# A fused four-layer kernel: the order of the first loads, and of the third pair's products

## What is computed

```
x = x + x @ W0[id0[b]] + b0[id0[b]]                      # one of 16 experts
x = x + x @ W1.T + s[a] * (x @ A[a].T) @ Bm[a].T          # W1, and one of 8 adapters, a = id1[b]
x = x + attention(x)                                      # see below
x = x + (W3[id3[b]] over the token axis) + b3[id3[b]]     # one of 8 subject matrices
```

## Time and profile before

| | |
|---|---|
| median of 3 runs | 934.08 us (932.72 to 934.34) |
| profiled execution: its time | 935.61 us |
| profiled execution: its span | 933.8 us |
| mean granted TensorE clock | 0.991 |
| TensorE busy | 890.7 us, 95% of the span |
| VectorE, ScalarE, GpSimd busy | 648.5, 442.8, 529.0 us |

### The profile page before, as it was taken

One profiled execution on the slowest core, in us unless ns is written; L12 is line 12 of the kernel. 1 busy time (PEld: TensorE's weight loads), 2 busy tenths in 40 slices (PEclk: granted clock), 3 DMA queues, 4 the chain that ended last, 5 costly groups with the idle time before them and its releaser, 6 DMA issues.

```text
span 933.8 us, 23545 instructions
## 1 busy us (share of the span) xinstructions
PE 890.7 (95%) x6501; PEld 654.8 (70%) x6501; DVE 648.5 (69%) x1858; ACT 442.8 (47%) x1190; POOL 529.0 (57%) x499
## 2 busy tenths in 40 slices
PE   5599999999999999999996899999999999999997
PEld 3357667666666676676676677878778778777785
DVE  3545445778787764466755778888778887787874
ACT  1424333333333333333423666666666676666762
POOL 2044655655746557865467666655666656666630
PEclk9889999999999999999999999999999999999999
DMA  9999988787887978887716766676766776666741
GB/s 285 300 285 333 332 303 294 258 286 258 264 291 241 295 252 273 307 269 263 250 64 214 209 205 193 194 211 189 214 194 193 210 222 206 198 199 202 227 133 47
DMA packets 100417, 218.55 MB, mean 234 GB/s; under 512 B 30187, under 2 KB 36168, under 8 KB 92178
## 3 DMA queue, kind: packets, MB, share of 16 engines
q1 hardware_dynamic: 66290, 145.27, 47.4%
q0 software_dynamic: 25088, 57.74, 21.5%
q10 hardware_dynamic: 8992, 15.00, 4.4%
HBM read 210.39 MB, written 33.86 MB: 262 GB/s over the span
## 4 chain that ended last, share of the span: by engine, by line
PE 77%; DVE 7%; DMA 6%; SPq 3%; issue 3%; ACTq 2%; ACT 2%; POOL 1%; DVEq 0%; POOLq 0%
PE banks L697 14%; PE banks L847 9%; PE banks L610 9%; PE banks L799 9%; PE banks L835 7%; PE banks L822 6%; PE banks L678 5%; PE banks L776 4%; DMA pair_b<-in_lb 4%; PE banks L883 3%; PE banks L840 3%; DVE later L1166 2%; PE banks L663 2%; PE banks L777 1%; PE banks L815 1%
## 5 line engine op out<-in xcount | busy, mean ns | idle before, releaser
L569 POOL DMA_INDIRECT ring<-new_rows,idx x128 | 129.3, 1010 | 81.1 <-PE banks L799 45.8
L1050 ACT ACTIVATE big<-big,neg_max 128x320 f32<-128x320 f32 x256 | 141.5, 555 | 4.7 <-DVE neg_max L1417 4.4
L1417 DVE CUSTOM_DVE_ANT_0 big<-banks,mask 128x320 f32<-128x320 f32 x256 | 114.6, 486 | 23.6 <-PE banks L799 22.5
L610 PE MATMUL banks<-ring 128*64 128x512 f32 x512 | 119.5, 609 | 11.5 <-DMA ring<-in_w 11.5
L497 POOL TENSOR_TENSOR rms<-ss,neg_half 128x12 f32<-128x12 f32 x30 | 68.5, 2283 | 70.3 <-DVE ss L1356 70.3
L1040 ACT ACTIVATE kt<-banks 128x384 f32<-128x384 f32 x128 | 61.8, 483 | 92.9 <-PE banks L777 92.8
L495 POOL TENSOR_TENSOR ring<-ring 128x512 f32<-128x512 f32 x30 | 38.7, 1291 | 87.4 <-DVE ring L1237 87.4
L558 POOL DMA_INDIRECT ring<-new_rows,idx x64 | 61.5, 961 | 47.0 <-PE banks L822 42.7
L799 PE MATMUL banks<-kt,q_in 64*128 64x128 f32 (+2 forms) x768 | 86.7, 358 | 1.3 <-ACT kt L1040 1.3
L1454 DVE TENSOR_SCALAR big<-big,recip 128x320 f32<-128x320 f32 x256 | 85.7, 397 | 2.3
L610 PEld LDWEIGHTS banks<-ring 128*64 128x64 f32 x512 | 35.0, 140 | 68.8 <-issue 67.5
(11 more groups left out here) (172 smaller groups left out, 2011.3 us busy)
## 6 DMA issues: line engine op xcount, KB each, us to landing
ring<-in_w SPq DMA_DIRECT2D x62, 1024.0 KB, 8.0
ring<-in_xt SPq DMA_DIRECT2D x32, 256.0 KB, 2.7
x_in<-in_x SPq DMA_DIRECT2D x32, 256.0 KB, 5.8
bias_in<-in_b SPq DMA_DIRECT2D x64, 128.0 KB, 8.0
x_dram<-x SPq DMA_DIRECT2D x32, 256.0 KB, 8.8
q_dram<-q_t ACTq DMA_DIRECT2D x32, 256.0 KB, 6.5
new_rows<-kv_out SPq DMA_DIRECT2D x32, 256.0 KB, 6.4
q_in<-q_dram SPq DMA_DIRECT2D x32, 256.0 KB, 2.8
```

Source lines behind the costliest of these rows:

```text
L569: pool.indirect_dma_start(out=kv[:, s, c, :], out_offset=None, in_=new_rows, in_offset=bass.IndirectOffsetOnAxis(ap=idx[:, b, 1 + c:2 + c] ...
L610: last = nc.tensor.matmul(ps_l0[T * h:T * h + T, :], xt[:, s, c, T * h:T * h + T], w0[:, 2 * s + h, c * D:(c + 1) * D], start=(c == 0), st ...
L1050: nc.scalar.activation(prob[:, s % 2, PLACE[g] * NK:(PLACE[g] + 1) * NK], sm[:, s % 2, g, :], ACT.Exp, bias=neg_max[:, s % 2, g:g + 1], sc ...
L1417: V.tensor_tensor_reduce(sm[:, s % 2, g, :], ps_s[g], mask[:, s % 2, k0:k0 + NK], 1.0, 3.0e38, ALU.add, ALU.min, accum_out=neg_max[:, s % ...
```

## The change

SyncE's first loads get another order. W1 goes ahead of the experts of pair 0; the rope loads of pairs 0 and 1 and all loads of pair 2 go ahead of Wq, Wk and Wv, so that phase_one of SyncE issues load_in from pair 3 on only. On ScalarE and VectorE the two parts of Wq, Wk and Wv are made in step 2 in place of step 1: on ScalarE behind x1t_hi and the x1t copy of pair 2 and ahead of the square of Q of pair 0, on VectorE behind split_x1 of pair 2 and ahead of rotate_parts. In step 2 TensorE transposes x1 and does the W1 product of pair 2 (transpose_x1, project_hidden) ahead of the Q product of pair 0. VectorE makes w1_lo ahead of x1 of pair 0. ScalarE gets a small copy at its start. The counts of the warm-up products change.

```diff
-WARM, WARM_X, WARM_T, WARM_Q, WARM_KEYS = 9, 6, 6, 24, 26
+WARM, WARM_X, WARM_T, WARM_Q, WARM_KEYS = 12, 6, 2, 24, 26
...
             sp.dma_start(xt[:, 0, :, :], a["xt"][0]).then_inc(ld_xt[0], 16)
+            sp.dma_start(w1_stage, a["w1"]).then_inc(ld_w1, 16)
             sp.wait_ge(ld_ids, 16)
...
-                sp.dma_start(w1_stage, a["w1"]).then_inc(ld_w1, 16)
                 sp.dma_start(lora_a[:, :, :], a["la"]).then_inc(ld_la, 16)
                 load_in(1, 0, 1)
+                for k in range(2):
+                    load_rope(k, k)
+                load_in(2, 1, 0)
                 sp.dma_start(wqkv_stage[:, :, 0:D], a["wq"]).then_inc(ld_wq, 16)
                 sp.dma_start(wqkv_stage[:, :, D:D + 256], a["wk"]).then_inc(ld_wkv, 16)
                 sp.dma_start(wqkv_stage[:, :, D + 256:], a["wv"]).then_inc(ld_wkv, 16)
-                for k in range(2):
-                    load_rope(k, k)
...
             def phase_one(k, j, s):
-                if on(k, 0, NP):
+                if on(k, 3, NP - 3):
                     load_in(k, j, s)
...
+                third = isinstance(k, int) and k == 2
+                if third:
+                    transpose_x1(k, s)
+                    project_hidden(k)
                 if on(k, 2, NP):
                     project_q(k - 2)
-                transpose_x1(k, s)
+                if not third:
+                    transpose_x1(k, s)
...
-                project_hidden(k)
+                if not third:
+                    project_hidden(k)
...
             act.wait_ge(pb_set, 2)
+            act.wait_ge(pool_set, 2)
+            nc.scalar.activation(scol[:, 8:20], neg_half[:, :], ACT.Copy)
...
-                if on(k, 2, NP):
+                third = isinstance(k, int) and k == 2
+                if on(k, 2, NP) and not third:
                     square_q(k - 2)
...
-                if isinstance(k, int) and k == 1:
+                if third:
                     act.wait_ge(ld_wq, 16)
                     nc.scalar.activation(wqkv_hi[:, :, 0:D], wqkv_stage[:, :, 0:D], ACT.Copy).then_inc(w_hi_ready, 1)
+                    act.wait_ge(ld_wkv, 2 * 16)
+                    nc.scalar.activation(wqkv_hi[:, :, D:], wqkv_stage[:, :, D:], ACT.Copy).then_inc(w_hi_ready, 1)
+                    square_q(0)
...
-                add_x1(k, s)
                 if isinstance(k, int) and k == 0:
                     dve.wait_ge(w_hi_ready, 1)
                     V.tensor_tensor(w1_lo[:, :, :], w1_stage, w1_hi[:, :, :].bitcast(F32), ALU.subtract).then_inc(w1_lo_ready, 1)
+                add_x1(k, s)
...
+                third = isinstance(k, int) and k == 2
+                if third:
+                    split_x1(k)
+                    for i in range(2):
+                        split_inputs(i)
                 if on(k, 2, NP):
                     rotate_parts(k - 2, s, 0)
-                split_x1(k)
+                if not third:
+                    split_x1(k)
```

More of the change, by code:

```diff
@@ L1004, in phase_one @@
                     round_x2(k - 1, x2t_hi)
-                if isinstance(k, int) and k == 1:
-                    act.wait_ge(ld_wkv, 2 * 16)
-                    nc.scalar.activation(wqkv_hi[:, :, D:], wqkv_stage[:, :, D:], ACT.Copy).then_inc(w_hi_ready, 1)
                 if on(k, 2, NP):
@@ L1344, in phase_one @@
                     make_gains()
-                if isinstance(k, int) and k == 1:
-                    split_inputs(0)
                 if on(k, 1, NP):
                     split_x2(k - 1, x2t_hi, x2t_lo)
-                if isinstance(k, int) and k == 1:
-                    split_inputs(1)
                 if on(k, 2, NP):
```

## The result

The changed kernel takes 925.72 us (median of 6 runs, 923.73 to 928.62) against 934.00 for the kernel before in the same lot (6 runs, 932.72 to 936.61): ratio 0.9909, interval 0.9887 to 0.993. Two later lots with the same two kernels gave 927.01 against 934.16 (0.9932, 0.9906 to 0.9958) and 926.12 against 934.14 (0.9917, 0.9894 to 0.9941). The profiled executions took 925.46 (span 923.6) and 935.61 (span 933.8).

The account below looks back on a forecast made before the run. The start was taken as bound by transfers. Pair 3's experts 6.4 us earlier, less 0.6 for small waits, gave 5.8 off the profiled 935.61, so 929.8; median forecast 928.3, range 926.0 to 932.2 us.

Parts of the forecast that it names:

- the hole at the start: DMA engines underused from 4 to 6 us; W1 sent there was to save some 0.8 us of transfer time.
- x1 of pair 0: First instant followed: W1 loaded ahead was to delay it by 2.1 us, from 18.69 to 20.8.
- W1's preparation: Rounding and split done before x1, so the first W1 product starts at 23.0 and is over by 27.6.
- Experts of pair 1: Their weights were to land at 28.0 and they to start at 28.3 instead of 30.38.
- Experts of pair 2: Weights landing at 40.5, start at 40.7 instead of 47.37, pause before them cut from 7.58 to 3.0 us.
- The clock at the third experts: Rival: clock falls again in the pause before pair 2's experts, costing 1.5 to 2.8 us, 929.8 to 931.1; chance 0.26.
- The step of pair 2 in its new order: From pair 2's experts to pair 3's: 16.9 us against 16.6 before, with Wq's rounding and split setting the pace.
- E3: Start of pair 3's experts on TensorE, forecast at 57.6 against 63.97, 6.4 us earlier.
- the rival of the late pair 3: Pair 3's weights, queued behind Wk and Wv, land at 61.2; time 932.1, or 934 with fallen clock; chance 0.12.
- E2: Start of pair 2's experts on TensorE, forecast at 40.7 instead of 47.37, 6.7 us earlier.
- Behind the step: After pair 3's experts start: adapter loads come some 2.8 us later against TensorE; 0.6 us charged, bounds 0 and 1.6.
- the adapter loop: Rival: ScalarE's late adapter loads delay every later step, 15 us over 28 steps, giving 943; chance 0.06.

Follow-up runs that it names:

- second trace of before: Kernel before, unchanged, profiled again: 934.63 us, ratio 1.0006.
- ropes first: Kernel before with only the four rope loads of pairs 0 and 1 moved ahead of Wq, Wk and Wv: 935.29 us, ratio 1.0008.
- extra load: Changed kernel with a second, unused copy of W1 (1024 KB) loaded ahead of pair 2's loads: 929.39 us, ratio 0.9957.
- late split: Changed kernel with the Q and K and V products waiting for the split's low part only ahead of the products that need it: 926.71 us, ratio 0.9915.
- loads only: Kernel before with all loads and W1's preparation as changed, but the matrices' rounding, splitting and products in the old order: 930.76 us, ratio 0.9965.
- after, again: Changed kernel, unchanged, profiled a second time: 927.01 us, ratio 0.9932.

## Why the prediction was right, and where it was wrong

The step that failed is the landing of pair 2's weights: forecast 40.5, with an early bound of 39.2, measured 35.2, 36.1 and 36.3. The mechanism held, loads that are needed first and go first; two transfer terms in it were sized too small, the hole at the start and the stretch from pair 1's weights to pair 2's. A gain of over 8 us, which came, had been given 0.04, and even there pair 2 stood at 39.2.

**x1 of pair 0** was forecast at 20.8 and came at 18.80 (18.69 before), earlier than its bounds allowed. Timelines of GpSimd and VectorE after:

```profile
17.44 1.26 POOL L469 TENSOR_TENSOR x_in<-x_in,bias_in 128x512 f32<-128x512 f32 x1 [8.59 <-DMA bias_in<-in_b]
...
18.80 0.69 DVE L1294 TENSOR_TENSOR x<-banks,x_in 128x512 f32<-128x512 f32 x1 [2.99 <-POOL x_in L469]
```

In both profiled executions x1 waits for GpSimd's sum of x and bias (the earlier trace rows and here), and that for the last bias of pair 0, which landed at 17.2 before and at 17.4 after. So 1024 KB of W1 ahead of pair 0 cost 0.2 us between these two and not 2.1 (that bias landed at 16.4 to 17.5 in the four traces with the old start, at 17.1 to 17.8 in the nine with W1 first): most of W1 went through the hole, which had been sized at 0.8 of its 2.9 us. The second half of the experts started 0.56 us later than before (15.29 against 14.73) and ended at the same time (17.75 and 17.73), so it did not matter. In the second trace of before those experts ended last, and x1 came at 19.59.

**W1's preparation** was right in its mechanism. The first W1 product (20.98) waited 0.33 us for its transposed input and not for a split. It was over at 24.0 where 27.6 was forecast: it started 2.0 us earlier and took 3.0 us, not the slow 4.5 of before.

**Experts of pair 1**: forecast 28.3, measured 25.98, 26.75 and 26.09. Their weights were forecast at 28.0 and landed at 25.8, 26.5 and 25.9; in every kernel that sends W1 early it is 25.6 to 26.5, against 27.9 to 29.1 in the four that leave the start as it was. Filling the hole was sized at 0.8 us and is worth 1.4 to 3.5. At the start 188 GB/s was compared with the 294 of later, but with W1 early the same two microseconds moved 419, and from 2 to 12 us the rate was 322 to 338 GB/s instead of 271 to 288.

**Experts of pair 2** were forecast at 40.7 and came at 35.39, 36.33 and 36.48. The working subtracted 5.8 and 0.8 from the 47.13 of one trace. 2.2, 1.5 and 2.1 us of the miss are pair 1's, the hole of the step before. The rest, 3.1, 2.9 and 2.1, is the stretch behind pair 1: forecast 12.5 us from pair 1's last weights to pair 2's (28.0 to 40.5), measured 9.4, 9.6 and 10.4. By subtraction the forecast kept what that stretch had of extra time in the trace that was read (11.7 us from Wv to pair 2, against 10.6 in the second trace of before and 9.4 to 10.7 in three other kernels that leave pair 2 behind Wv). The 9.1 us that pair 3 took after pair 2 stood in the text as a bound; behind the 25.8 to 26.5 measured for pair 1 they give 34.9 to 35.6. In the bound of 39.2 they left 30.1 for pair 1 and the ropes, where the last rope landed at 26.9 to 27.5; and the value taken was the farther one. Why the stretch is longer behind the three matrices stays open, as said at ropes first.

**The clock at the third experts**: with the weights there at 35.2, the forecast pause of 3.0 us was 0, 0 and 0.93 us, and the clock stayed full. The rival did not occur; extra load, with its pause of 2.80, suggests that at the forecast pause it would have. Shorter pauses went either way ahead of pair 1's experts: behind 1.82 and 1.89 us (late split and loads only) the low level followed, and the experts took 5.35 us, behind 1.91 (after, again) it did not, and they took 3.65.

**The step of pair 2 in its new order** was right: forecast 16.9, measured 17.11, 17.08 and 17.10. Wq's split was wanted 10.35 us after the experts' start, and the Q product started 10.46 after it (45.85). Its last wait was 1.05, with 0.78 and 0.27 ahead of the W1 product's parts, where 1.6 was forecast at one place. So the step is longer than before (63.80 - 47.37 = 16.43 by the timeline, 15.41 in the second trace), and the gain is all ahead of it.

**Pair 3's weights** landed at 50.7 to 51.9, ahead of E3 at 52.50 to 53.58: the rival of the late pair 3 did not occur. Its experts came 4.0 to 5.1 us ahead of the forecast 57.6, which is the miss of E2.

**Behind the step** 0.6 us was charged. E3 to the next experts is 14.06, 14.36 and 14.92, against 14.02 before: 0 to 0.9, right. The rounding of the adapter rows was forecast 8.2 us after E3 (10.1 less the 1.9 behind it) and came 8.44, 8.74 and 9.26 after it. From E3 to the last but one group of experts on the chain in this phase takes 373.3 and 373.0 us in the two traces of before and 372.8, 373.1 and 374.2 after. So the adapter loop, the rival of the other sign, did not occur, and the lead is carried through but for about 1 us in the third trace of after.

**The sum.** Between the two profiled executions E3 leads by 11.3 us and the attention's first key transposes by 12.1 (494.87 against 507.01), but the end only by 10.15. The 2 us are the low clock in the attention: from the first key transposes to the end of the span takes 426.7 to 426.9 us in the nine traces whose clock is full there, 428.2 to 430.0 in the other five, and the second trace of before is one of these (428.9). Two of the five traces with the old order of pair 2's loads have it and three of the nine with the new one, so nothing ties it to the change. Against that second trace the three of after lead at the key transposes by 9.9, 8.5 and 7.3 us, close to what the medians show (8.3, 7.2, 8.0). That the time missed by only 2.6 us where E2 missed by 4.2 to 5.3 is luck: the trace of before that E3 was counted from was itself 2 us late there, and counted from the second trace the forecast lead of 6.4 us would be 4.3. The forecast's mechanism was right, and so were the terms behind E2; the two transfer terms at the start, about 2 and 2 to 3 us, were sized too small.

## What to carry to other kernels

Before subtracting from one trace's landing time, build it up as well from the shortest comparable stretch in the trace, and take the second profile of the same kernel where there is one: where they differ by 2 us, that is the term's uncertainty. Where loads are re-ordered, follow each queue that consumes them: with the loads moved alone, ScalarE and VectorE stood at the matrices that now came late, and more than half of the gain was gone. A hole in the DMA at the very start is worth filling, with a load that is needed early anyhow. Before a term is given to an instant such as x1, look up in the timeline what it waits for: here it was a bias and not the weights.

## What was not expected

The attention's first batches can run at half clock. In the trace after the stretch is 10.2 us long; in the first trace of before there is none. The window of that trace at the same place:

```profile
507.00:517.00 10.00, 6.09 (x46) 4.69 (x47) 4.61 (x20) 4.62 (x13) 7.41 (x8) 1.00 0.54 147
```

Of the three traces of after one had 10.2 us of it, one 13.7 at 497.1, and one only 3.4 at 489.7, ahead of the attention; of the two of before one had none and one 10.2 us. The 1.00 in the window above is what the forecast was read from. What decides which it is was not found; the extra products in the waits ahead of it did not.

The same 1024 KB of W1 cost 0.2 us at the last bias of pair 0 (between the two profiled executions), sent into the hole at the start, and 1.7 to 2.8 at pair 2's last weights, sent into a busy queue (extra load).
